# Two attention stages: the order of VectorE's work around the softmax maximum, and ScalarE for the last step of the layer norm

## The chip, the cores and the metric

The kernel runs on one core of a Trainium2 chip. It is one program with six stages. The metric is the device time of one execution in microseconds (us), the median of several runs. The engines of the core run side by side, each through its own instruction list in order, and wait for each other with semaphores: PE (TensorE, matmuls; PEld is its weight load), DVE (VectorE), ACT (ScalarE), POOL (GpSimd), and SP, which issues DMAs.

## The reference

32 batches of 128 rows of 128 values pass through six blocks; after each of them the block's output is added to its input and layer-normed without gain or bias. Two of the blocks are softmax attentions with 16 heads of 8 values, and the change is in these two:

```python
# stage 1: self-attention with rotary positions and a causal mask
scores = jnp.einsum('bhqd,bhkd->bhqk', Q, K) * scale
scores = jnp.where(causal_mask, -jnp.inf, scores)
attn = jax.nn.softmax(scores, axis=-1)
...
x = _layernorm(x + _L0_attn_ref(x, ...), axis=-1)
...
# stage 5: cross-attention, 77 keys from ctx_1024, a bias table and a padding mask
probs = jax.nn.softmax(scores, axis=-1)
out = jnp.einsum('bhts,bhsd->bhtd', probs, v)
...
x = _layernorm(x + _L1_xattn_ref(x, ctx_1024, ...), axis=-1)

def _layernorm(x, axis=-1, eps=1e-05):
    m = jnp.mean(x, axis=axis, keepdims=True)
    v = jnp.var(x, axis=axis, keepdims=True)
    return (x - m) / jnp.sqrt(v + eps)
```

## The kernel before

One function, `attention`, writes both stages; `cross` tells them apart (tile names begin with `a_` in the self-attention and `k_` in the cross-attention). The 32 batches are worked in 8 groups of 4, and the softmax of a group in 8 units: a unit is 8 heads of one batch, 128 query rows with 8 x 128 scores (self) or 8 x 77 scores (cross). I write "unit 0'" for a unit of the next group.

A unit passes through the engines like this. PE computes the scores into one of two pairs of PSUM banks (L660, in the self-attention with a mask added by L663). DVE takes the row maximum `mx` (L481) and subtracts it into `DD` (L483), so that the bank pair is free. ACT takes the exponential `E` (L370). PE transposes it (L670), ACT copies the transposed probabilities `PT` out of PSUM (L411), and PE multiplies them with the values for each batch (L680). DVE also sums each unit's exponentials into `sm` (L492); in the self-attention POOL first folds the two halves of `E` into `HS` (L280). The scores of unit u + 2 stand behind the transposes of unit u in PE's list, so each unit's chain feeds the next but one.

At the end of a group DVE takes the reciprocal `rr` of all 64 sums (L550), POOL spreads it to `rx` (L356), PE transposes that (L743), ACT copies it (L461), DVE multiplies it with the output into `oT` (L565), PE projects (L754), and DVE adds the residual into `Y` (L572), takes mean and variance (L72, L75), and, after POOL has computed the reciprocal deviation `rs` (L82, L84), writes the normed rows into `X` (L90, `ln_apply`: four instructions of 128 x 128).

No scheduler is involved. The order of each engine's list is the order in which `prelude` and `body` issue it; `schedule` (L223) runs the groups, the first two of the cross-attention written out, then pairs in a loop, then the last two. Beside the softmax, each group prepares the next one: transposed rows, projected keys, queries and values (in the self-attention with four rotary products `R` on DVE, L504; in the cross-attention with ACT writing the queries in four pieces `QM`, L400). In the cross-attention each group also computes the router logits of the group before: PE transposes its normed rows (L625), ACT copies them (L392), PE multiplies (L632), and DVE writes them to `LA` (L497).

Of the kernel before, what the change touches and what calls it, by code (L numbers as in the profile page):

```python
# [20 lines left out]
P = 128  # L21
# [80 lines left out]

LN_SEMS = "st mv lv rs"
# [62 lines left out]
def attention(c, tag, cross, W, wsem, wcount, xsem=None, first=None, gate=None):  # L166
# [11 lines left out]
    s = c.sems(tag, "xs xTp xT kp rot q k bd vp v z zv s_ready mx ma d e sm rr ex rTp ptp pt o_ready oT yp yr y2 xw cs cTp cT rc qf bf bl ql pf pw pd hs xTl xL lg la " + LN_SEMS)  # L178
# [44 lines left out]
    def schedule(eng, prelude, body):  # L223

        prelude()
        if cross and eng is nc.tensor:
            for g in range(NG):
                body(g, g % 2, min(2, NG - 1 - g))
            return
        if cross:  # L230
            body(0, 0, 2)
            body(1, 1, 2)
        with eng.Fori(1 if cross else 0, NG // 2 - 1) as i:
            body(i * 2, 0, 2)
            body(i * 2 + 1, 1, 2)
        body(NG - 2, 0, 1)
        body(NG - 1, 1, 0)
# [4 lines left out]
    with nc.Block() as block:  # L242
# [27 lines left out]
        def _(pool):  # L270
# [58 lines left out]
            def body(g, par, left):  # L329
# [31 lines left out]
                ln_rstd(pool, nc, ln, s, g + 1)  # L361
# [4 lines left out]
        def _(act):  # L366
# [53 lines left out]

            def prelude():
                if first is not None:
                    first["act"](act)
                nc.scalar.preload_act_table_set("exp_and_others")
                act.sem_inc(s["o_ready"], 1)
                if cross:
                    act.wait_ge(wsem, wcount)
                    nc.scalar.copy(QM[:, 0].rearrange("p g (b q) -> p g b q", b=GB), W["qc"][:, :, :].rearrange("p g (o q) -> p g o q", o=1).to_broadcast([D, 4, GB, P])).then_inc(s["qf"], 1)
                x_transposed(0)
                act.wait_ge(wsem, wcount)  # L430
                if cross:
# [12 lines left out]

            def body(g, par, left):
                for u in range(1, UN):
                    slot(g, u, left)
                    if left:
# [7 lines left out]
                        elif u == 6:  # L456
                            values(g + 1, 1 - par)
                    if cross and u == 5 and earlier(g):
# [11 lines left out]
        def _(dve):  # L470

            def less_max(g, par, u):
                hf, b = u % 2, u // 2
                at = g * UN + u + 1
                d = DD[:, u % 2].rearrange("p (i j) k -> p i j k", i=2)
                m = mx[:, u % 2, :].rearrange("p (i j) -> p i j", i=2)
                mb = mx[:, u % 2, :].rearrange("p (i j o) -> p i j o", i=2, o=1).to_broadcast([P, 2, HG, KL])
                dve.wait_ge(s["s_ready"], at)
                if not (isinstance(g, int) and g == 0 and u < 2):
                    dve.wait_ge(s["e"], at - 2)  # L480
                nc.vector.tensor_reduce(m, units(hf), AX_X, ALU.max).then_inc(s["mx"], 1)  # L481
                dve.wait_ge(s["mx"], at)
                nc.vector.tensor_tensor(d, units(hf), mb, ALU.subtract).then_inc(s["d"], 1)  # L483
# [30 lines left out]
            def prelude():  # L514
# [19 lines left out]
                less_max(0, 0, 0)  # L534
                less_max(0, 0, 1)
                sums(0, 0)
                less_max(0, 0, 2)
                sums(0, 1)
                if not cross:
                    rotate(1, 0)  # L540
# [848 lines left out]
def state_space(c, W, wsem, wcount, Wr, rsem, rcount):  # L1389
# [40 lines left out]
    ln, iln = c.ln, {k: (c.sb("m_i" + k, v.shape, F32, ctx) if k not in ("half", "eps") else v) for k, v in c.ln.items()}  # L1430
# [856 lines left out]
def program(nc, dram, out):  # L2287
    ctx = ExitStack()
    with ctx:
# [6 lines left out]
                "rs": c.sb("ln_rs", [P, GB]), "half": c.sb("ln_half", [P, GB]), "eps": c.sb("ln_eps", [P, GB])}  # L2296
# [39 lines left out]
        def first_dve(dve):  # L2336
            nc.vector.memset(c.warm[:, :], 1.0).then_inc(s_warm, 1)
            nc.vector.memset(c.ln["eps"][:, :], EPS)
            nc.vector.memset(c.ln["half"][:, :], -0.5)

# [123 lines left out]
```

## Time and profile before

| what | value |
|---|---|
| median of 3 runs | 1926.71 us (1925.93 to 1927.08) |
| span of the profiled execution | 1948.6 us; its own time is given only as this span, 21.9 us (1.1%) above the median of the runs |
| PE busy | 1562.9 us (80%) |
| DVE busy | 1491.3 us (77%) |
| ACT busy | 953.5 us (49%) |
| POOL busy | 920.7 us (47%) |
| self-attention, one group in the middle | 34.9 to 35.0 us (eight groups, from 0 to 308 us) |
| cross-attention, one group in the middle | 29.2 to 29.3 us (eight groups, from 1298 to 1556 us) |

The profile is one execution of the program taken by the hardware profiler. Busy shares over the whole span say little, since the six stages have different limits. The two stages of the change together take about 570 us of the span. A group is measured here from the start of one addition of the residual (`Y`, L572) to the next.

### The profile page before, as it was taken

Reading aid. Unit: us, or ns where it says so; the run is one execution under the profiler, and the core shown is the slowest. Engines: PE = TensorE matmul, PEld = TensorE weight load, DVE = VectorE, ACT = ScalarE, POOL = GpSimd, SP = SyncE. Lnnn points to the kernel's source line nnn. Section 1 sums busy time; section 2 is a strip of 40 time slices with the busy share of each in tenths; the row PEclk is TensorE's granted clock in tenths of the full one; section 3 lists DMA queues with packets and bytes.
Section 4 is the critical chain, followed back from the end, with each engine's and each line's share of the span. In section 5 each row is a group of like instructions: output and inputs, shape, how many; then the busy total and the mean of one; then the engine's idle time right before and its main releaser. Section 6 shows DMA issues by size and latency. Waiting matters only on the chain. (4 is left out here: it accounts for less than half of the span.)

```text
span 1948.6 us, 31799 instructions
## 1 busy us (share of the span) xinstructions
PE 1562.9 (80%) x10219; PEld 1017.4 (52%) x10219; DVE 1491.3 (77%) x2947; ACT 953.5 (49%) x1491; POOL 920.7 (47%) x938
## 2 busy tenths in 40 slices
PE   8889888989699978977878878769998811699991
PEld 4545547988476632322333333236776611588891
DVE  6899986887488779999989999967777678533335
ACT  3545543575544567657656666436566410011114
POOL 4455442444200147677676677654344100366653
PEclk8999998999899989999988999979999855799996
DMA  4000000000000000000000000020000040466654
GB/s 144 2 0 0 0 1 27 2 2 1 12 1 0 1 1 1 1 1 0 0 1 0 0 0 1 1 78 11 5 9 5 3 145 0 159 209 206 212 171 135
DMA packets 49075, 75.34 MB, mean 39 GB/s; under 512 B 8861, under 2 KB 34821, under 8 KB 48437
## 3 DMA queue, kind: packets, MB, share of 16 engines
q1 hardware_dynamic: 43541, 64.12, 10.5%
q0 software_dynamic: 4544, 9.32, 1.6%
q8 instruction: 67, 1.10, 0.2%
q14 instruction: 59, 0.48, 0.1%
q10 hardware_dynamic: 864, 0.33, 0.1%
HBM read 62.26 MB, written 11.48 MB: 38 GB/s over the span
## 5 line engine op out<-in xcount | busy, mean ns | idle before, releaser
L1506 POOL TENSOR_TENSOR m_hC<-m_h,m_Cs 128x512 f32<-128x512 f32 x256 | 328.2, 1287 | 169.2 <-DVE m_h L1680 122.6
L1788 PE MATMUL PS<-m_hC,identf 128*128 128x512 f32 x512 | 296.5, 662 | 100.9 <-POOL m_hC L1506 99.9
L1680 DVE TENSOR_TENSOR_SCAN m_h<-m_dA,PS 128x512 f32<-128x512 f32 x256 | 312.4, 1220 | 11.2
L1788 PEld LDWEIGHTS PS<-m_hC,identf 128*128 128x128 f32 x512 | 93.0, 203 | 236.4 <-POOL m_hC L1506 208.9
L1675 DVE TENSOR_TENSOR PS<-PS,m_DU 128x512 f32<-128x512 f32 x256 | 178.4, 697 | 19.9 <-issue 3.8
L1616 ACT ACTIVATE m_dA<-m_DT,m_A 128x508 f32<-128x508 f32 x256 | 174.3, 714 | 31.3 <-DVE m_DT L1664 31.1
L1996 ACT ACTIVATE e_Sg<-PS 128x512 f32<-128x512 f32 x71 | 42.4, 597 | 223.0 <-PE PS L2238 178.8
L2238 PE MATMUL PS<-e_xT,e_WT 128*128 128x128 f32 x1136 | 143.8, 281 | 4.9 <-DVE e_xT L2146 3.4
L1608 ACT COPY m_Cs<-PS 128x512 f32<-128x512 f32 x128 | 73.7, 576 | 143.7 <-PE PS L1766 143.5
L2238 PEld LDWEIGHTS PS<-e_xT,e_WT 128*128 128x128 f32 x1136 | 135.4, 195 | 9.3 <-DVE e_xT L2146 7.1
L1935 POOL DMA_INDIRECT e_XG<-token_rows,e_ids x71 | 68.8, 969 | 138.9 <-DVE e_ids L2140 117.6
L2153 DVE TENSOR_TENSOR e_HT<-PS,e_Sg 128x512 f32<-128x512 f32 x71 | 49.0, 691 | 81.6 <-PE PS L2238 73.5
L82 POOL TENSOR_TENSOR ln_lv<-ln_mv,ln_eps 128x4 f32<-128x4 f32 x24 | 4.8, 200 | 223.9 <-DVE ln_mv L75 223.9
L280 POOL TENSOR_TENSOR a_HS<-a_E 128x512 f32<-128x512 f32 x56 | 71.2, 1271 | 74.7 <-ACT a_E L370 74.7
L1940 POOL DMA_INDIRECT expert_rows<-e_Yo,e_ids x71 | 70.0, 985 | 72.2 <-DVE e_Yo L2159 60.6
L411 ACT COPY a_PT<-PS 128x1024 f32<-128x1024 f32 x63 | 63.8, 1012 | 73.8 <-PE PS L670 73.8
L411 ACT COPY k_PT<-PS 77x1024 f32<-77x1024 f32 x63 | 63.5, 1008 | 67.7 <-PE PS L670 67.5
L370 ACT ACTIVATE a_E<-a_DD 128x1024 f32<-128x1024 f32 x64 | 67.7, 1058 | 54.1 <-DVE a_DD L483 53.6
L670 PE MATMUL PS<-identf,a_E 128*128 128x128 f32 x512 | 71.6, 285 | 22.6 <-ACT a_E L370 22.3
L303 POOL TENSOR_TENSOR k_BD<-k_kT,w_hmask 32x1232 f32<-32x1232 f32 x32 | 71.5, 2233 | 36.3 <-ACT k_kT L387 30.4
L481 DVE TENSOR_REDUCE a_mx<-PS 128x8 f32<-128x1024 f32 x64 | 77.4, 1210 | 11.8 <-PE PS L663 11.6
L660 PE MATMUL PS<-k_BD,k_QM 128*128 128x308 f32 x256 | 80.8, 439 | 4.1 <-POOL k_BD L303 2.2
(411 smaller groups left out, 3801.6 us busy)
## 6 DMA issues: line engine op xcount, KB each, us to landing
e_WT<-in_w_wgu SPq DMA_DIRECT2D x71, 512.0 KB
token_rows<-X SPq DMA_DIRECT2D x2, 2048.0 KB
e_Y<-expert_rows SPq DMA_DIRECT2D x16, 256.0 KB, 4.0
k_BD<-in_w_bcr SPq DMA_DIRECT2D x1, 2464.0 KB, 9.5
e_w_wd<-in_w_wd SPq DMA_DIRECT2D x1, 2048.0 KB, 7.9
out_dram<-X SPq DMA_DIRECT2D x8, 256.0 KB, 2.4
X<-in_x SPq DMA_DIRECT2D x1, 1792.0 KB, 8.7
x_Cs<-in_ctx SPq DMA_DIRECT2D x8, 154.0 KB
```

The costliest lines, as they stand in the source:

```text
L303: nc.gpsimd.tensor_tensor(BD[r, par, gp].rearrange("p j b k -> p j (b k)"), flat(kT[r, :, :]).rearrange("p (o n) -> p o n", o=1).to_broadc ...
L411: nc.scalar.copy(PT[:, u % NP], PS[0:KL, 4:6, :].rearrange("p i (h q) -> p (i h) q", q=P)).then_inc(s["pt"], 1)
L481: nc.vector.tensor_reduce(m, units(hf), AX_X, ALU.max).then_inc(s["mx"], 1)
L660: ins = nc.tensor.matmul(scores(gp), q, BD[r, par, gp, :, b, :] if cross else BD[r, par, :, b, :], start=True, stop=cross)
L670: ins = nc.tensor.transpose(PS[0:KL, 4 + h // 4, (h % 4) * P:(h % 4 + 1) * P], E[:, u % NE, h, :], c.identf[:, :])
L1506: nc.gpsimd.tensor_tensor(hC[:, i % ND, :], hst[:, i % ND, :], Cs[:, n % ND, :], ALU.mult).then_inc(s["hC"], 1)
L1608: nc.scalar.copy(Cs[:, n % ND, :], bank(3)).then_inc(s["Cs"], 1)
L1616: nc.scalar.activation(dA[:, i % NA, :, 1:P], bl(DT[:, par, ch, :])[:, :, 1:P], ACT.Exp, scale=A[:, ch, n:n + 1]).then_inc(s["dA"], 1)
L1675: nc.vector.tensor_tensor(bank(4), bank(1 + n % 2), DU[:, par, ch, :], ALU.mult).then_inc(s["dBu"], 1)
L1680: nc.vector.tensor_tensor_scan(hst[:, i % ND, :], dA[:, i % NA].rearrange("p b l -> p (b l)"), bank(4), 0.0, ALU.mult, ALU.add).then_inc(s ...
L1788: nc.tensor.matmul(bank(5 + ch), c.identf[:, :], hC[:, i % ND, :], start=False, stop=(n == NS - 1)).then_inc(s["yacc"], 1)
L2238: ins = nc.tensor.matmul(PS[:, banks[i % 2], f * P:(f + 1) * P], WT[:, i % RW, w, f * P:(f + 1) * P], xT[:, i % 2, :], start=True, stop=True)
```

## The change

`less_max` is split. A new `maximum` takes the row maximum, and `less_max` is left with the subtraction, which now also carries the wait for the exponential of two units earlier. Between the two, VectorE's list now holds other work: in the self-attention a rotary product and the sums of an earlier unit, in the cross-attention the sums. The sums of unit u - 1 move from behind the subtraction of unit u to ahead of that of unit u + 1. At the end of a group the maximum of unit 0' is taken ahead of the last two sums.

The last step of the layer norm, `ln_apply` on VectorE, becomes `norm` on ScalarE (scale by `rs`, bias by `nb`) for all groups but the last. It is issued in the group after, behind the exponential of unit 4. GpSimd's `ln_scale` computes the additional `nb` = -mean x `rs` with two more operations on 128 x 4 values. VectorE waits for ScalarE (`xw`) before it writes `Y` again. The self-attention's first two groups are now also written out ahead of the loop.

```diff
+def ln_scale(pool, nc, ln, s, n):
+    pool.wait_ge(s["mv"], n)
+    nc.gpsimd.tensor_tensor(ln["lv"][:, :], ln["mv"][:, :, 1], ln["eps"][:, :], ALU.add).then_inc(s["lv"], 1)
+    nc.gpsimd.tensor_tensor(ln["ng"][:, :], ln["mv"][:, :, 0], ln["minus"][:, :], ALU.mult).then_inc(s["ng"], 1)
+    pool.wait_ge(s["lv"], n)
+    nc.gpsimd.tensor_tensor(ln["rs"][:, :], ln["lv"][:, :], ln["half"][:, :], ALU.pow).then_inc(s["rs"], 1)
+    pool.wait_ge(s["rs"], n)
+    pool.wait_ge(s["ng"], n)
+    nc.gpsimd.tensor_tensor(ln["nb"][:, :], ln["ng"][:, :], ln["rs"][:, :], ALU.mult).then_inc(s["nb"], 1)
...
-        if cross:
-            body(0, 0, 2)
-            body(1, 1, 2)
-        with eng.Fori(1 if cross else 0, NG // 2 - 1) as i:
+        body(0, 0, 2)
+        body(1, 1, 2)
+        with eng.Fori(1, NG // 2 - 1) as i:
...
-                ln_rstd(pool, nc, ln, s, g + 1)
+                if left:
+                    ln_scale(pool, nc, ln, s, g + 1)
+                else:
+                    ln_rstd(pool, nc, ln, s, g + 1)
...
+            def norm(g):
+                act.wait_ge(s["nb"], g + 1)
+                for b in range(GB):
+                    ins = nc.scalar.activation(X[:, bass.ds(g * GB + b, 1), :].rearrange("p o d -> p (o d)"), Y[:, b, :], ACT.Identity, scale=ln["rs"][:, b:b + 1], bias=ln["nb"][:, b:b + 1])
+                ins.then_inc(s["xw"], 1)
...
+                    if u == 3 and earlier(g):
+                        norm(g - 1)
...
-            def less_max(g, par, u):
+            def maximum(g, u):
+                dve.wait_ge(s["s_ready"], g * UN + u + 1)
+                nc.vector.tensor_reduce(mx[:, u % 2, :].rearrange("p (i j) -> p i j", i=2), units(u % 2), AX_X, ALU.max).then_inc(s["mx"], 1)
+            def less_max(g, u):
...
             def body(g, par, left):
-                for u in range(2, UN):
-                    if u + 1 < UN:
-                        less_max(g, par, u + 1)
-                        sums(g, u)
-                    else:
-                        sums(g, u)
-                        dve.wait_ge(s["sm"], g * UN + UN)
-                        nc.vector.reciprocal(rr[:, :], sm[:, :]).then_inc(s["rr"], 1)
-                        if left:
-                            less_max(g + 1, 1 - par, 0)
-                            less_max(g + 1, 1 - par, 1)
-                    if left:
-                        if cross:
-                            if u == 5:
-                                values(g + 1, 1 - par)
-                        elif u <= 4:
-                            rotate(g + 1, u - 1)
+                for u in range(2, UN - 1):
+                    maximum(g, u + 1)
+                    if left and not cross and u <= 5:
+                        rotate(g + 1, u - 2)
+                    if u >= 3:
+                        sums(g, u - 1)
+                    less_max(g, u + 1)
+                    if left and cross and u == 5:
+                        values(g + 1, 1 - par)
                     if cross and u == 6 and earlier(g):
                         logits(g - 1)
+                if left:
+                    maximum(g + 1, 0)
+                sums(g, UN - 2)
+                sums(g, UN - 1)
+                dve.wait_ge(s["sm"], g * UN + UN)
+                nc.vector.reciprocal(rr[:, :], sm[:, :]).then_inc(s["rr"], 1)
+                if left:
+                    less_max(g + 1, 0)
+                    maximum(g + 1, 1)
+                    less_max(g + 1, 1)
...
+                if earlier(g):
+                    dve.wait_ge(s["xw"], g)
                 nc.vector.tensor_tensor(flat(Y[:, :, :]), bank(AUX), flat(XB[:, :, :] if cross else group(c, g)), ALU.add).then_inc(s["yr"], 1)
                 dve.wait_ge(s["yr"], g + 1)
                 ln_stats(dve, nc, Y, ln, s, g + 1)
                 if left:
-                    less_max(g + 1, 1 - par, 2)
+                    maximum(g + 1, 2)
                     sums(g + 1, 1)
-                    if left == 2 and not cross:
-                        rotate(g + 2, 0)
-                ln_apply(dve, nc, group(c, g), Y, ln, s, g + 1, s["xw"])
+                    less_max(g + 1, 2)
+                else:
+                    ln_apply(dve, nc, group(c, g), Y, ln, s, g + 1, s["xw"])
```

Three places of the instruction lists are shown, all in the second group of the cross-attention, which is written out in both kernels.

The first is on VectorE at the end of a group, from the subtraction of unit 7 on. `LA` is the logits of the group before, the `k_sm` rows are the sums, the `k_rr` row is the reciprocal, and the `k_mx` and `k_DD` rows behind it belong to units 0' and 1'. Before:

```order
L483 TENSOR_TENSOR k_DD<-PS,k_mx 128x616
L492 TENSOR_REDUCE k_sm<-k_E 128x8
L497 TENSOR_SCALAR LA<-PS 128x32
L492 TENSOR_REDUCE k_sm<-k_E 128x8
L550 RECIPROCAL k_rr<-k_sm 128x64
L481 TENSOR_REDUCE k_mx<-PS 128x8
L483 TENSOR_TENSOR k_DD<-PS,k_mx 128x616
L481 TENSOR_REDUCE k_mx<-PS 128x8
L483 TENSOR_TENSOR k_DD<-PS,k_mx 128x616
```

The same place on VectorE after the change:

```order
L505 TENSOR_TENSOR k_DD<-PS,k_mx 128x616
L519 TENSOR_SCALAR LA<-PS 128x32
L497 TENSOR_REDUCE k_mx<-PS 128x8
L514 TENSOR_REDUCE k_sm<-k_E 128x8 x2
L582 RECIPROCAL k_rr<-k_sm 128x64
L505 TENSOR_TENSOR k_DD<-PS,k_mx 128x616
L497 TENSOR_REDUCE k_mx<-PS 128x8
L505 TENSOR_TENSOR k_DD<-PS,k_mx 128x616
```

Between the logits and the reciprocal there was one sum; now there are the maximum of unit 0' and two sums.

The second place is on VectorE behind the statistics of the layer norm, with the maximum and the subtraction of unit 2' and the sums of unit 1'. Before:

```order
L72 BN_STATS ln_st<-k_Y 128x6 x4
L75 BN_AGGR ln_mv<-ln_st 128x2 x4
L481 TENSOR_REDUCE k_mx<-PS 128x8
L483 TENSOR_TENSOR k_DD<-PS,k_mx 128x616
L492 TENSOR_REDUCE k_sm<-k_E 128x8
L90 TENSOR_SCALAR X<-k_Y,ln_mv,ln_rs 128x128 x4
```

The same place on VectorE after the change:

```order
L72 BN_STATS ln_st<-k_Y 128x6 x4
L75 BN_AGGR ln_mv<-ln_st 128x2 x4
L497 TENSOR_REDUCE k_mx<-PS 128x8
L514 TENSOR_REDUCE k_sm<-k_E 128x8
L505 TENSOR_TENSOR k_DD<-PS,k_mx 128x616
```

The sums of unit 1' moved ahead of the subtraction of unit 2', and the four instructions that write `X` are gone.

The third place is on ScalarE, behind the copy `k_PT` of unit 3 and the exponential `k_E` of unit 4. Before:

```order
L411 COPY k_PT<-PS 77x1024
L370 ACTIVATE k_E<-k_DD 128x616
L400 ACTIVATE k_QM<-PS,w_bq 32x512 x4
L411 COPY k_PT<-PS 77x1024
L370 ACTIVATE k_E<-k_DD 128x616
```

The same place on ScalarE after the change:

```order
L425 COPY k_PT<-PS 77x1024
L384 ACTIVATE k_E<-k_DD 128x616
L414 ACTIVATE k_QM<-PS,w_bq 32x512 x4
L439 ACTIVATE X<-k_Y,ln_nb,ln_rs 128x128 x4
L425 COPY k_PT<-PS 77x1024
L384 ACTIVATE k_E<-k_DD 128x616
```

The four new instructions stand between the four query pieces and the copy of unit 4, with the exponential of unit 5 behind that.

## Rows read from the trace of the kernel before

**Rows 1.** The head of the page: the span of the profiled execution.

```profile
span 1948.6 us, 31799 instructions
```

**Rows 2.** Stretches, a group each: length, busy PE PEld DVE ACT POOL, granted clock, DMA.

```profile
165.10:200.08 34.98, 31.53 (x272) 17.83 (x272) 32.04 (x44) 17.89 (x19) 18.11 (x18) 1.00 0.00 0
1348.10:1377.40 29.30, 26.41 (x268) 20.86 (x268) 23.14 (x44) 18.35 (x25) 13.04 (x9) 1.00 0.03 8
1406.66:1435.89 29.23, 26.42 (x268) 20.84 (x268) 23.14 (x44) 18.34 (x25) 13.03 (x9) 1.00 0.03 7
```

**Rows 3.** Waits over five cross-attention groups: total us, times, longest.

```profile
DVE LA L497 <- PE PS L632: 7.2, 5, 1.5
```

**Rows 4.** Timeline of VectorE in a cross-attention group: start, duration, instruction, idle before.

```profile
1408.63 0.77 DVE L481 TENSOR_REDUCE k_mx<-PS 128x8 f32<-128x616 f32 x1
1409.43 0.80 DVE L483 TENSOR_TENSOR k_DD<-PS,k_mx 128x616 f32<-128x616 f32 x1
1410.14 0.78 DVE L492 TENSOR_REDUCE k_sm<-k_E 128x8 f32<-128x616 f32 x1
1410.85 1.11 DVE L90 TENSOR_SCALAR X<-k_Y,ln_mv,ln_rs 128x128 f32 x4
...
1428.52 0.19 DVE L497 TENSOR_SCALAR LA<-PS 128x32 f32 x1 [1.44 <-PE PS L632]
1428.63 0.79 DVE L492 TENSOR_REDUCE k_sm<-k_E 128x8 f32<-128x616 f32 x1
1429.44 0.55 DVE L550 RECIPROCAL k_rr<-k_sm 128x64 f32<-128x64 f32 x1
```

**Rows 5.** Timeline of TensorE in the same group: transposes of units 2 and 5, of `rx`.

```profile
1411.12 1.07 PE L670 MATMUL PS<-identf,k_E 128*77 128x128 f32 x8 [0.88 <-ACT k_E L370]
...
1422.57 1.10 PE L670 MATMUL PS<-identf,k_E 128*77 128x128 f32 x8
...
1431.29 0.60 PE L743 MATMUL PS<-identf,k_rx 128*128 128x128 f32 x4
```

**Rows 6.** Timeline of ScalarE in the same group: queries, copy of unit 4, exponential of unit 5.

```profile
1417.72 2.75 ACT L400 ACTIVATE k_QM<-PS,w_bq 32x512 f32<-32x512 f32 x4 [0.27 <-PE PS L609]
1420.50 1.01 ACT L411 COPY k_PT<-PS 77x1024 f32<-77x1024 f32 x1
1421.53 0.72 ACT L370 ACTIVATE k_E<-k_DD 128x616 f32<-128x616 f32 x1
```

**Rows 7.** Timeline of ScalarE in stage 4, where it norms rows.

```profile
796.54 1.50 ACT L1630 ACTIVATE X<-PS,m_no,ln_rs 128x128 f32 x4 [1.87 <-POOL m_no L1516]
797.92 1.33 ACT L1616 ACTIVATE m_dA<-m_DT,m_A 128x508 f32<-128x508 f32 x2
```

**Rows 8.** Timeline of GpSimd in the same cross-attention group.

```profile
1430.08 1.04 POOL L356 TENSOR_TENSOR k_rx<-k_rr,k_one 128x512 f32<-128x512 f32 x1 [4.73 <-DVE k_rr L550]
```

**Rows 9.** Timeline of VectorE in a self-attention group.

```profile
135.73 2.19 DVE L90 TENSOR_SCALAR X<-a_Y,ln_mv,ln_rs 128x128 f32 x4
...
154.65 0.68 DVE L492 TENSOR_REDUCE a_sm<-a_HS 128x8 f32<-128x512 f32 x1
156.08 1.22 DVE L492 TENSOR_REDUCE a_sm<-a_E 128x8 f32<-128x1024 f32 x1 [0.76 <-ACT a_E L370]
157.34 0.55 DVE L550 RECIPROCAL a_rr<-a_sm 128x64 f32<-128x64 f32 x1
157.81 1.16 DVE L481 TENSOR_REDUCE a_mx<-PS 128x8 f32<-128x1024 f32 x1
```

**Rows 10.** Timeline of TensorE in the same self-attention group.

```profile
141.45 1.09 PE L670 MATMUL PS<-identf,a_E 128*128 128x128 f32 x8 [1.13 <-ACT a_E L370]
...
154.96 0.60 PE L663 MATMUL PS<-w_cmask,identb 128*128 128x512 bf16 x2
...
161.37 1.09 PE L670 MATMUL PS<-identf,a_E 128*128 128x128 f32 x8 [0.64 <-ACT a_E L370]
```

**Rows 11.** Timeline of TensorE in the last cross-attention group.

```profile
1528.18 1.92 PE L670 MATMUL PS<-identf,k_E 128*77 128x128 f32 x8 [2.58 <-ACT k_E L370]
```

More of the change, by code:

```diff
@@ L177, in attention @@
     EXPERTS, SK_EPS = 8, 0.05
-    s = c.sems(tag, "xs xTp xT kp rot q k bd vp v z zv s_ready mx ma d e sm rr ex rTp ptp pt o_ready oT yp yr y2 xw cs cTp cT rc qf bf bl ql pf pw pd hs xTl xL lg la " + LN_SEMS)
+    s = c.sems(tag, "xs xTp xT kp rot q k bd vp v z zv s_ready mx ma d e sm rr ex rTp ptp pt o_ready oT yp yr y2 xw cs cTp cT rc qf bf bl ql pf pw pd hs xTl xL lg la ng nb " + LN_SEMS)
     ctx = ExitStack()
@@ L470, in _ @@
         def _(dve):
-            def less_max(g, par, u):
-                hf, b = u % 2, u // 2
+            def maximum(g, u):
+                dve.wait_ge(s["s_ready"], g * UN + u + 1)
+                nc.vector.tensor_reduce(mx[:, u % 2, :].rearrange("p (i j) -> p i j", i=2), units(u % 2), AX_X, ALU.max).then_inc(s["mx"], 1)
+            def less_max(g, u):
                 at = g * UN + u + 1
-                d = DD[:, u % 2].rearrange("p (i j) k -> p i j k", i=2)
-                m = mx[:, u % 2, :].rearrange("p (i j) -> p i j", i=2)
                 mb = mx[:, u % 2, :].rearrange("p (i j o) -> p i j o", i=2, o=1).to_broadcast([P, 2, HG, KL])
-                dve.wait_ge(s["s_ready"], at)
                 if not (isinstance(g, int) and g == 0 and u < 2):
                     dve.wait_ge(s["e"], at - 2)
-                nc.vector.tensor_reduce(m, units(hf), AX_X, ALU.max).then_inc(s["mx"], 1)
                 dve.wait_ge(s["mx"], at)
-                nc.vector.tensor_tensor(d, units(hf), mb, ALU.subtract).then_inc(s["d"], 1)
+                nc.vector.tensor_tensor(DD[:, u % 2].rearrange("p (i j) k -> p i j k", i=2), units(u % 2), mb, ALU.subtract).then_inc(s["d"], 1)
             def sums(g, u):
@@ L533, in prelude @@
                     dve.wait_ge(xsem[1], 16)
-                less_max(0, 0, 0)
-                less_max(0, 0, 1)
+                maximum(0, 0)
+                less_max(0, 0)
+                maximum(0, 1)
+                less_max(0, 1)
+                maximum(0, 2)
                 sums(0, 0)
-                less_max(0, 0, 2)
+                less_max(0, 2)
                 sums(0, 1)
-                if not cross:
-                    rotate(1, 0)
             def body(g, par, left):
-                for u in range(2, UN):
-                    if u + 1 < UN:
-                        less_max(g, par, u + 1)
-                        sums(g, u)
-                    else:
-                        sums(g, u)
-                        dve.wait_ge(s["sm"], g * UN + UN)
-                        nc.vector.reciprocal(rr[:, :], sm[:, :]).then_inc(s["rr"], 1)
-                        if left:
-                            less_max(g + 1, 1 - par, 0)
-                            less_max(g + 1, 1 - par, 1)
-                    if left:
-                        if cross:
-                            if u == 5:
-                                values(g + 1, 1 - par)
-                        elif u <= 4:
-                            rotate(g + 1, u - 1)
+                for u in range(2, UN - 1):
[7 more added lines that the diff above has]
+                        values(g + 1, 1 - par)
                     if cross and u == 6 and earlier(g):
                         logits(g - 1)
+                if left:
[8 more added lines that the diff above has]
+                    less_max(g + 1, 1)
                 dve.wait_ge(s["rc"], g + 1)
@@ L1429, in state_space @@
     hC = sb("hC", [P, ND, T])
-    ln, iln = c.ln, {k: (c.sb("m_i" + k, v.shape, F32, ctx) if k not in ("half", "eps") else v) for k, v in c.ln.items()}
+    ln, iln = c.ln, {k: (c.sb("m_i" + k, v.shape, F32, ctx) if k not in ("half", "eps") else v) for k, v in c.ln.items() if k not in ("ng", "nb", "minus")}
     bank = lambda i, r=P: PS[0:r, i, :]
@@ L2295, in program @@
         c.ln = {"st": c.sb("ln_st", [P, GB, 6]), "mv": c.sb("ln_mv", [P, GB, 2]), "lv": c.sb("ln_lv", [P, GB]),
-                "rs": c.sb("ln_rs", [P, GB]), "half": c.sb("ln_half", [P, GB]), "eps": c.sb("ln_eps", [P, GB])}
+                "rs": c.sb("ln_rs", [P, GB]), "ng": c.sb("ln_ng", [P, GB]), "nb": c.sb("ln_nb", [P, GB]), "minus": c.sb("ln_minus", [P, GB]), "half": c.sb("ln_half", [P, GB]), "eps": c.sb("ln_eps", [P, GB])}
         c.PS = ctx.enter_context(nc.psum_tensor("PS", [P, 8, 512], F32))
@@ L2339, in first_dve @@
             nc.vector.memset(c.ln["half"][:, :], -0.5)
+            nc.vector.memset(c.ln["minus"][:, :], -1.0)
         def first_pe(pe):
```

## The prediction, made before the changed kernel ran

> **What bounds the kernel now.** I read the head of the page first [rows 1]: the profiled execution spans 1948.6 us, 21.9 us more than the median of the runs. The sum below is made of differences between stretches of this execution, and I set it against the median one to one, since the two stages' groups repeat to a tenth of a us. A measurement of this kernel can tell some 0.2% (3.9 us) from no change.
>
> Next the busy time by stretch [rows 2]. The reader should see how different the two stages are. A self-attention group takes 34.98 us, of which VectorE works 32.04 and TensorE 31.53: both are close to full. A cross-attention group takes 29.23 us; there TensorE works 26.42 and VectorE only 23.14. VectorE has 6 us of idle time in it, TensorE 2.8. The granted clock is 1.00 (2.4 GHz) in all three, and the second stretch, written out in straight lines, is no slower than the third, a pass of the loop, by more than 0.07 us; so I cost the two self-attention groups that are now written out at nothing.
>
> Then the list of waits in the cross-attention: VectorE waits 1.4 to 1.5 us in each group for the router logits before it may write `LA` [rows 3]. Last the timelines of one group, engine by engine, to see which wait ends last. TensorE's row of the `rx` transposes shows no wait in it [rows 5]: TensorE runs without a pause from the transposes of unit 6 to the end of the group, so what makes TensorE late in this stage makes the group late. That is the test for each edit.
>
> **The change in the cross-attention.** Three moved pieces can reach TensorE.
>
> First, the sums of unit 1' now stand ahead of the subtraction of unit 2'. Before, the maximum began at 1408.63 and the subtraction at 1409.43 [rows 4]. The subtraction (0.80 long) is followed by independent work 0.71 after its start, while a maximum of about the same length holds its reader for 0.80: the separation is worth 0.09. The new order puts the maximum (0.77, so 0.69 until the next starts) and the sums (0.71) ahead: 1408.63 + 0.69 + 0.71 = 1410.03, so the subtraction comes 0.60 later. Its exponential, and the transposes of unit 2, are waited for by TensorE already (0.88 at 1411.12 [rows 5]), and everything behind them in TensorE's list moves too. **+0.6 per group.**
>
> The Trainium skill, in "VectorE: DVE Perf Modes", section "The DRAIN you can't avoid", says that VectorE flushes after every operation and that a semaphore between chained operations costs nothing extra; by this, standing other work between saves nothing, and the term would be 0.7. The trace's 0.09 disagrees with it here, by little.
>
> Second, ScalarE's new step. It is the same operation as stage 4's, scale and bias from a column each, on 128 x 128, four times: 1.50 us, and the next instruction starts 1.38 after its start [rows 7]. That one reads PSUM and this one SBUF, which the row does not show. From below I bound it by VectorE's four instructions for the same work, 1.11 [rows 4], from above by four without overlap: each overlaps the next by 1.50 - 1.38 = 0.12, so 1.38 + 4 x 0.12 = 1.86. I take 1.38, the nearest row. It stands behind the four query pieces, which end at 1420.47, and ahead of the copy of unit 4, which began at 1420.50 with no idle time before it [rows 6]: ScalarE is already late there. Behind the copy is the exponential of unit 5, which ended at 1421.53 + 0.72 = 1422.25, and TensorE took that unit's transposes at 1422.57 without a wait [rows 5]. The slack is 0.27 after the 0.05 of a hand-over. 1.38 - 0.27: **+1.1 per group.**
>
> Third, the reciprocal. VectorE wrote `LA` at 1428.52, then one sum, and took the reciprocal at 1429.44 [rows 4]. Now the maximum of unit 0' (0.71) and a further sum (0.71) stand between, because they follow the logits, whose wait does not get shorter: TensorE issues them late. The reciprocal comes 1.42 later. GpSimd's `rx` follows it, 1430.08 to 1431.12 [rows 8], and TensorE transposed that at 1431.29 [rows 5]: slack 0.12 after the hand-over. **+1.3 per group.** What is late next hangs on TensorE: the transposed reciprocals, the product `oT`, the projection, `Y`. The subtraction of unit 0' comes only 0.65 later than before and hides behind that.
>
> These three add, since each delays TensorE from a point at which it then runs on or waits in order: 3.0 us in each of the six intervals in which a group's logits, queries and successor all exist, 18.0 us. The first and the last group have neither the second nor the third (no logits or no queries), but the first: 0.3 to 0.6 each, 0.9 together. VectorE's 1.02 of `ln_apply` (1410.85, 1.11 long [rows 4]) comes off an engine that then waits for TensorE: nothing. The new wait of VectorE for ScalarE ahead of `Y` is over more than 10 us earlier; behind it stands the whole layer norm, so it would cost its full length if the cover went. GpSimd's two more small operations delay only its copy of rows, and it waited 4.73 us in front of `rx` [rows 8].
>
> **The change in the self-attention.** VectorE gives up 2.19 per group [rows 9] and some 0.09 in each of seven separated pairs. TensorE is the one to ask again. It waited 1.13 for the exponential of unit 3 [rows 10], behind `ln_apply`: that wait goes. The subtraction of unit 2' comes 0.5 later, as above (sums of 0.68, less the overlap and the 0.09). TensorE is 0.6 ahead from there and runs on without a wait until the scores of unit 0', which ended at 154.96 + 0.60 = 155.56 and now end at 154.9. VectorE now takes the maximum of unit 0' there (1.1 until the next starts), then the sums of unit 6 (0.6) and those of unit 7 (1.26 until the reciprocal may start, 156.08 to 157.34 [rows 9]): the reciprocal is at 157.9, 0.5 later than before. So the lead is lost at `rx`. Afterwards TensorE no longer waits its 0.64 for the exponential of unit 0' [rows 10], whose subtraction now follows the reciprocal at once instead of after the maximum (157.81). 0.64 - 0.5 leaves 0.1 to 0.3; I take 0.2, seven times: **-1.4.** The bounds: both waits recovered, 1.77 per group; or nothing. ScalarE's new step lies in a stage where ScalarE is busy 17.89 of 34.98 [rows 2], and I put it at nothing; if it were uncovered it would cost 1.38 per group.
>
> **Sum.** 18.0 + 0.9 - 1.4 = +17.5 us: 1926.7 + 17.5 = 1944.2 us, 0.9% slower.
>
> **The rivals.**
>
> VectorE is the bound in both stages (faster). Then what is taken off it comes off the time: 2.1 and 0.6 in seven self-attention groups, 1.0 and 0.6 in seven cross-attention groups, 30 us, 1896 us. For it speaks VectorE's 32.04 of 34.98; against it the 23.14 of 29.23 [rows 2]. It decides at TensorE's idle time: if that does not grow beyond 2.8 us in a cross-attention group, this one is right. Chance 0.07. The Trainium skill, in "Perfetto Trace Analysis", section "Optimizing Scalar/DVE Operations", says that where VectorE is saturated, giving work to ScalarE may make sense; by that rule's condition the trace agrees in the self-attention only.
>
> The cross-attention's delays fall into the 2.8 us in which TensorE waits anyway (no change): 1926.7 - 1.4 = 1925.3 us. Against it: at the transposes of unit 5 and of `rx` there is no wait to fall into [rows 5]. Chance 0.07.
>
> The self-attention recovers both of TensorE's waits: 1.77 instead of 0.2, seven times, 11 us better, 1933.2 us. For it: VectorE has nearly 3 us less to do. Against it: the reciprocal stands behind a maximum that waits for scores. Chance 0.12.
>
> The clock falls. After a wait of 2.58 us TensorE's transposes took 1.92 instead of 1.1 in the last group [rows 11], that is 1.2 GHz; the scores behind them double too, some 1.7 us for one such dip. The longer waits of TensorE could bring one in each of six groups: +10, 1954.4 us. Against it: each single wait stays below 1.6 us, and the waits of 0.88 and 1.13 left the clock at 1.00 [rows 2]. Chance 0.10.
>
> **How the numbers follow.** My forecast has 0.64, with a range of its own of 1938 to 1949: ScalarE's step at 1.11 or 1.86 gives -1.6 or +2.9 in six groups, the self-attention's ends +1.4 or -3 within this case. The predicted time is 1944.2. The range, to take in the recovery in the self-attention and nearly all of the clock's case, is 1933 to 1954. Slower by over 0.2%: 0.64 + 0.12 + 0.10 = 0.86; within 0.2%: 0.07; faster: 0.07.
>
> **What the profile after would show.** Middle groups of the cross-attention of about 32.2 us instead of 29.2, of the self-attention of about 34.8. TensorE waiting about 1.5 us for the exponential of unit 2 and about 1 us each for that of unit 5 and for `rx`, where there was 0.88, nothing and nothing. ScalarE's four instructions at about 1.5 us, right between the queries and a copy that does not wait. VectorE idle for 8 us or more in a cross-attention group. The prediction is wrong if ScalarE's step turns out far shorter than 1.1, if the logits come early enough for the reciprocal, or if self-attention groups fall to 33 us.

## The result, and the profile after

The changed kernel takes **1945.93 us** (median of 4, 1944.83 to 1950.64) against 1926.89 us (median of 4, 1925.93 to 1929.99) for the kernel before on the same chip: ratio 1.0104, 95% interval 1.0093 to 1.0116, 1.0% slower. The forecast was 1944.2 us, 1933 to 1954.

The two profiled spans can't be compared: the first execution of the kernel before [rows 1] spent 396.9 us behind its last `Y`, where every other profile here has 369 to 373. So I compare the stretches between additions of the residual (`Y`), in two profiles of each kernel:

| stretch, us | before | after |
|---|---|---|
| a middle self-attention interval | 34.9 to 35.0 | 34.45 to 34.73 |
| last self-attention interval | 33.90, 35.50 | 35.47, 35.46 |
| a middle cross-attention interval | 29.23 to 29.31 | 32.45 to 32.58 |
| last cross-attention interval | 28.08, 28.10 | 31.11, 31.12 |
| all seven of the self-attention | 243.5, 245.0 | 242.5, 242.5 |
| all seven of the cross-attention | 203.62, 203.66 | 226.25, 226.25 |

The seven intervals of the cross-attention lose 22.6 us, those of the self-attention give back 0.9 to 2.5. The first cross-attention group, which no interval holds, loses 0.8: from its first transposes of `E` to its `Y` it took 30.93 and 30.99 us before, and 31.78 twice after. That makes 20.9 to 22.5 us, more than the 19.0 between the medians. Where the other 2 to 3.5 us came back is not shown: the stretch from the self-attention's last `Y` to the cross-attention's first, nearly all of it stages that the change doesn't touch, took 1040 to 1050 us in the profiles of this study.

The windows of the profile after, with the columns of [rows 2], are a stretch as long as a self-attention group, a cross-attention group and the last cross-attention interval:

```profile
165.59:200.05 34.46, 31.33 (x273) 17.91 (x272) 29.25 (x39) 19.12 (x23) 18.44 (x20) 1.00 0.00 0
1414.95:1447.48 32.53, 26.68 (x268) 20.78 (x268) 21.58 (x40) 19.97 (x29) 13.36 (x11) 1.00 0.02 7
1545.05:1576.16 31.11, 24.94 (x229) 19.28 (x229) 17.30 (x31) 13.44 (x19) 3.77 (x6) 0.79 0.00 1
```

In the cross-attention group VectorE works 1.6 us less and idles 11 us; TensorE does the same work in 3.3 us more, and its idle time grows from 2.8 to 5.9 us. Its timeline in that group has the three waits (the last bracket) where [rows 5] had 0.88, none and none:

```profile
1419.99 1.07 PE L697 MATMUL PS<-identf,k_E 128*77 128x128 f32 x8 [1.45 <-ACT k_E L384]
...
1432.81 1.07 PE L697 MATMUL PS<-identf,k_E 128*77 128x128 f32 x8 [1.30 <-ACT k_E L384]
...
1442.82 0.66 PE L770 MATMUL PS<-identf,k_rx 128*128 128x128 f32 x4 [1.16 <-POOL k_rx L367]
```

VectorE's timeline shows the cause of the first and the third, to be read against [rows 4]: the sums between maximum and subtraction, and the maximum and two sums between `LA` and the reciprocal.

```profile
1416.92 0.77 DVE L497 TENSOR_REDUCE k_mx<-PS 128x8 f32<-128x616 f32 x1
1417.60 0.78 DVE L514 TENSOR_REDUCE k_sm<-k_E 128x8 f32<-128x616 f32 x1
1418.30 0.79 DVE L505 TENSOR_TENSOR k_DD<-PS,k_mx 128x616 f32<-128x616 f32 x1
...
1438.73 0.19 DVE L519 TENSOR_SCALAR LA<-PS 128x32 f32 x1 [1.57 <-PE PS L659]
1438.86 0.80 DVE L497 TENSOR_REDUCE k_mx<-PS 128x8 f32<-128x616 f32 x1
1439.58 1.49 DVE L514 TENSOR_REDUCE k_sm<-k_E 128x8 f32<-128x616 f32 x2
1441.10 0.55 DVE L582 RECIPROCAL k_rr<-k_sm 128x64 f32<-128x64 f32 x1
```

ScalarE's timeline shows the cause of the second, to be read against [rows 6]: the norm holds the copy of unit 4 and the exponential of unit 5 back by 1431.04 - 1429.37 = 1.67 us.

```profile
1426.59 2.75 ACT L414 ACTIVATE k_QM<-PS,w_bq 32x512 f32<-32x512 f32 x4 [0.27 <-PE PS L636]
1429.37 1.65 ACT L439 ACTIVATE X<-k_Y,ln_nb,ln_rs 128x128 f32 x4
1431.04 1.01 ACT L425 COPY k_PT<-PS 77x1024 f32<-77x1024 f32 x1
1431.95 0.72 ACT L384 ACTIVATE k_E<-k_DD 128x616 f32<-128x616 f32 x1
```

### The profile page after: what moved, and what is told of

Read it like the earlier page. It is cut to its first block and busy times, and to the rows that moved or that the text cites. A ratio compares the mean times of both kernels' runs of the same rounds, so it can differ in the third digit from the quotient of the medians.

```text
span 1947.8 us, 31764 instructions
## 1 busy us (share of the span) xinstructions
PE 1555.3 (80%) x10219; PEld 1016.8 (52%) x10219; DVE 1462.8 (75%) x2892; ACT 973.9 (50%) x1547; POOL 925.3 (48%) x966
## 3 DMA queue, kind: packets, MB, share of 16 engines
q8 instruction: 71, 1.16, 0.2%
## 5 line engine op out<-in xcount | busy, mean ns | idle before, releaser
L1643 ACT ACTIVATE m_dA<-m_DT,m_A 128x508 f32<-128x508 f32 x256 | 174.3, 714 | 34.3 <-DVE m_DT L1691 31.1
L497 DVE TENSOR_REDUCE k_mx<-PS 128x8 f32<-128x616 f32 x64 | 50.8, 793 | 62.7 <-PE PS L687 62.6
L697 PE MATMUL PS<-identf,k_E 128*77 128x128 f32 x512 | 71.6, 285 | 23.9 <-ACT k_E L384 23.9
```

The source lines that it names most:

```text
L497: nc.vector.tensor_reduce(mx[:, u % 2, :].rearrange("p (i j) -> p i j", i=2), units(u % 2), AX_X, ALU.max).then_inc(s["mx"], 1)
L697: ins = nc.tensor.transpose(PS[0:KL, 4 + h // 4, (h % 4) * P:(h % 4 + 1) * P], E[:, u % NE, h, :], c.identf[:, :])
L1643: nc.scalar.activation(dA[:, i % NA, :, 1:P], bl(DT[:, par, ch, :])[:, :, 1:P], ACT.Exp, scale=A[:, ch, n:n + 1]).then_inc(s["dA"], 1)
```

## The experiments

The theory: three separate delays of TensorE (late subtraction, norm on ScalarE, late reciprocal) make the cross-attention slow, and they add. Against it: one of them alone, ScalarE's added work as such, or VectorE as the bound. Group times are those of middle groups. A ratio is to the kernel before, with its 95% interval.

**Each part alone.** `order_only` has the new order with the norm back on VectorE (and GpSimd's `ln_rstd` in every group); against the changed kernel:

```diff
...
-                    if u == 3 and earlier(g):
-                        norm(g - 1)
...
-                if earlier(g):
-                    dve.wait_ge(s["xw"], g)
...
-                else:
-                    ln_apply(dve, nc, group(c, g), Y, ln, s, g + 1, s["xw"])
+                ln_apply(dve, nc, group(c, g), Y, ln, s, g + 1, s["xw"])
```

`norm_only` has the old order with the norm on ScalarE (with GpSimd's `ln_scale`, and the first two self-attention groups written out as in the change); against the kernel before:

```diff
...
+                    if u == 3 and earlier(g):
+                        norm(g - 1)
...
+                if earlier(g):
+                    dve.wait_ge(s["xw"], g)
...
-                ln_apply(dve, nc, group(c, g), Y, ln, s, g + 1, s["xw"])
+                else:
+                    ln_apply(dve, nc, group(c, g), Y, ln, s, g + 1, s["xw"])
```

> VectorE's new order alone; the last step of the layer norm is back on VectorE in every group, ScalarE has none of it. My theory (TensorE is made late at three separate places of a middle cross-attention group: 0.57 us at the transposes of unit 2, 1.37 at those of unit 5, 1.28 at those of the reciprocals): the first and the third remain, the second goes, so a cross-attention group takes about 31.1 us against 29.25 before and 32.5 after, and a self-attention group is not better than before (34.9 to 35.1), since there the reciprocal is later and the norm's 2.1 us are back on VectorE; time about 1941 to 1943 us. Rival S (all the loss comes from ScalarE's new step, the late reciprocal only follows from it): cross-attention groups of 29.3, time 1925 to 1928. Rival V (all the loss comes from VectorE's order): groups of 32.5, time 1946 or more.

> VectorE's order is that of before (maximum and subtraction side by side, sums behind), and ScalarE does the last step of the layer norm at the place of the change. My theory: in the cross-attention only the second delay remains, a middle group takes 30.3 to 30.6 us; in the self-attention VectorE gives up 2.2 us per group and its reciprocal is not later, so a group falls to about 33.6 us against 34.95 before and 34.5 after. Time 1922 to 1927 us. Rival S: cross-attention groups of 32.5, time 1940 or more. Rival V: cross-attention groups of 29.3.

Measured, `order_only`: 1933.21 us (ratio 1.0044, 1.0027 to 1.0062), cross group 31.1 to 31.2, self group 34.45. The cross-attention was as expected (29.25 + 1.9), the self-attention was not: the new order alone gives all of the 0.5 us. The time came 8 us below the expected 1941 to 1943. Part of that is the self-attention (about 0.5 us a group) and the last cross-attention interval, 27.64 us instead of the changed kernel's 31.11; the rest was not followed up. `norm_only`: 1924.16 us (0.9989, 0.9979 to 1.0000), cross 30.6 (29.25 + 1.35; one of 30.93), self 33.66 to 33.85, as expected. So in the self-attention the norm on ScalarE is worth 1.2 us in the old order and nothing in the new one (why: the last experiment).

**Each delay undone in the cross-attention alone**, against the changed kernel. `norm_early` issues the norm one unit earlier:

```diff
-                    if u == 3 and earlier(g):
+                    if u == (2 if cross else 3) and earlier(g):
```

`recip_back` puts the logits behind the sums of unit 6 and the maximum of unit 0' behind the reciprocal:

```diff
-                    if cross and u == 6 and earlier(g):
-                        logits(g - 1)
-                if left:
+                if left and not cross:
                     maximum(g + 1, 0)
                 sums(g, UN - 2)
+                if cross and earlier(g):
+                    logits(g - 1)
...
+                if left and cross:
+                    maximum(g + 1, 0)
```

`sum_behind` has the subtraction of unit 2' ahead of the sums of unit 1':

```diff
-                    sums(g + 1, 1)
-                    less_max(g + 1, 2)
+                    if cross:
+                        less_max(g + 1, 2)
+                        sums(g + 1, 1)
+                    else:
+                        sums(g + 1, 1)
+                        less_max(g + 1, 2)
```

`three_back` has all three edits.

> The change, but in the cross-attention ScalarE does the norm one unit earlier, behind the copy of the keys, where it waited 1.44 us for TensorE's transposes of unit 3; the self-attention is as in the change. My theory: the second delay goes (TensorE's transposes of unit 5 no longer wait), the two others remain: groups of 31.1 to 31.3 us, time about 1938 us. Rival S: groups of 29.3, time 1926. Rival V: groups of 32.5, time 1946.

> The change, but at the end of a cross-attention group VectorE's order is that of before: sums of unit 6, logits, sums of unit 7, reciprocal, and only then the maximum of unit 0 of the next group. My theory: the third delay goes (TensorE's transposes of the reciprocals no longer wait), groups of 31.2 us, time about 1938 us. Rival S: unchanged, groups of 32.5, time 1946. Rival V: groups of 30.0 or less, since only 0.6 of VectorE's new order is left.

> The changed kernel with the three subtractions and sums at the end of a cross group in the old order (subtraction of the next group's unit 2 ahead of the sums of its unit 1); nothing else differs. If the late subtraction is what makes TensorE wait for the transposes of unit 2, that wait falls from 1.45 to about 0.9 us, a middle cross group from 32.5 to 31.8 to 32.0 us, and the time from 1946 to 1941.5 to 1943 us. Rival, VectorE's own work sets the group: the order of two of its instructions changes nothing, the group stays at 32.5 us and the time at 1946 us.

> The changed kernel with all three suspected delays undone in the cross attention alone (subtraction before sums, reciprocal in its old place, ScalarE's norm one unit earlier); the norm stays on ScalarE and the self attention is as changed. If the three delays are the whole loss, a middle cross group is 29.2 to 29.5 us (before 29.25), a self group 34.45 to 34.7 us, and the time 1923 to 1928 us. Rival, the norm on ScalarE costs something by itself wherever it stands, since ScalarE has 1.65 us more to do in each group: the group stays at 30.5 us or more and the time at 1934 us or more.

| kernel | time, us | ratio to before | cross group, us | TensorE's three waits, us |
|---|---|---|---|---|
| after | 1945.93 | 1.0104 (1.0093 to 1.0116) | 32.5 | 1.45, 1.30, 1.16 |
| norm_early | 1938.73 | 1.0054 (1.0032 to 1.0075) | 31.2 | 1.45, none, 1.16 |
| recip_back | 1938.15 | 1.0055 (1.0038 to 1.0071) | 31.15 | 1.45, 1.31, none |
| sum_behind | 1942.14 | 1.0076 (1.0057 to 1.0094) | 32.0 | 0.95, 1.30, 1.15 |
| three_back | 1930.41 | 1.0004 (0.9990 to 1.0017) | 29.3 | 0.95, none, none |

Each edit takes away its own wait and leaves the others. They are worth 1.3, 1.4 and 0.5 us, and together 3.2: they add. A window of `three_back` has the group at 29.30 us, with ScalarE still doing the norm (19.75 us busy instead of 18.34):

```profile
1411.47:1440.77 29.30, 26.42 (x268) 20.84 (x268) 21.67 (x41) 19.75 (x29) 13.37 (x11) 1.00 0.03 7
```

So ScalarE's 1.4 us of added work cost nothing by themselves; their place did. `three_back`'s time missed the expected 1923 to 1928: its profiled execution (1933.49 us) took 1050.1 us between the two attentions' additions, where that of the changed kernel took 1045.2, and 30.59 in the last interval, below. Why the other runs are long too is not shown; the ten lie between 1923.1 and 1933.5.

**The last groups.** A piece is a row of TensorE's timeline, some matrix products of one kind. In the changed kernel's last cross-attention interval TensorE waits 3.37 us and then runs five pieces at 1.2 GHz. Before, the wait was 2.58 us [rows 11] and two pieces were slow:

```profile
1550.37 1.96 PE L697 MATMUL PS<-identf,k_E 128*77 128x128 f32 x8 [3.37 <-ACT k_E L384]
1552.12 2.26 PE L687 MATMUL PS<-k_BD,k_QM 128*128 128x308 f32 x4
1554.31 1.94 PE L707 MATMUL PS<-k_PT,k_V 77*32 77x128 f32 x32
1556.18 1.99 PE L697 MATMUL PS<-identf,k_E 128*77 128x128 f32 x8
1557.96 2.15 PE L687 MATMUL PS<-k_BD,k_QM 128*128 128x308 f32 x4
1559.97 1.07 PE L697 MATMUL PS<-identf,k_E 128*77 128x128 f32 x8
```

`warm_last` adds dummy products to that wait (and to the self-attention's) in TensorE's list of the changed kernel; two further runs repeat the kernels.

```diff
+                    if u == 2 and not left:
+                        pe.wait_ge(s["yr"], g)
+                        keep_warm(c, 14, AUX)
```

> The changed kernel, and in the last group of either attention TensorE does 14 dummy matrix products, into a bank that nobody reads, while it waits for the transposes of unit 2 (added work, the result is untouched). If the last intervals are long because TensorE's clock falls after the wait of 3.37 us, the granted clock of the last cross-attention interval rises from 0.79 to 0.95 or more, that interval falls from 31.1 to 26.5 to 27.5 us, the last self-attention interval from 35.5 to 31 to 33 us; the middle groups stay at 32.5 and 34.5 us; the time falls by 4 to 7 us to 1939 to 1942 us. Rival, the last groups are long by their order alone: the two intervals stay within 1 us and so does the time, or it grows by the products.

> The changed kernel once more, for one profile. If it is chance how many of TensorE's pieces run at 1.2 GHz after the wait in the last cross-attention group, that interval differs from the first profile's 31.1 us, anywhere from 26.3 to 31.5 us, while the middle groups repeat at 32.45 to 32.58 us. If the length of the wait alone sets it, the interval is 31.1 us again.

> The kernel before once more, for one profile. Middle groups 34.9 and 29.25 us again; the last cross-attention interval anywhere from 25.5 to 28.1 us if the slow pieces are chance, 28.1 us if they are set by the wait. The part behind the last Y of the cross-attention, 396.9 us in the first profile and 370 to 372 us in all the other kernels', should come to 370 us, and the span to about 1923 us.

`warm_last`: 1939.63 us (1.0062, 1.0046 to 1.0079). Its two last intervals:

```profile
270.18:301.71 31.53, 25.19 (x239) 14.95 (x240) 21.98 (x31) 15.33 (x18) 9.77 (x11) 0.94 0.00 1
1545.97:1573.17 27.20, 23.41 (x241) 17.50 (x243) 17.39 (x31) 13.34 (x19) 3.78 (x6) 0.96 0.01 2
```

That is 3.9 us less in each, at a clock of 0.94 and 0.96, with middle groups unchanged: the clock it is. How many pieces run slowly the length of the wait alone does not say. After 2.58 us `norm_only` had none slow, as its row shows; after 2.86 `three_back` had five, `sum_behind` two, the second of them in part:

```profile
1529.55 1.07 PE L696 MATMUL PS<-identf,k_E 128*77 128x128 f32 x8 [2.58 <-ACT k_E L384]
```

The repeated profiles gave 31.12 and 28.10 again in the cross-attention, but `before_again`'s last self-attention interval took 35.50 us where the first had 33.90: after the same wait of 3.29 us six pieces were slow instead of four. Its span was 1929.8 us, not the expected 1923 (the part behind the last `Y` was 372.8, near the expected 370). The Trainium skill, "TensorE: Matmul & The Clock Gate", section "Part 1: The HAM clock gate (the "warmup" mystery)", says of a kernel's start that the number of slow matmuls varies between runs of one kernel. The 33.90 and 35.50 are a like difference behind a wait, and the two equal pairs don't show one.

**A version that beats both.** `no_early` is the old order with the norm on ScalarE, in the cross-attention a unit earlier; `best2` adds the dummy products of `warm_last`. `no_early` against `norm_only`:

```diff
-                    if u == 3 and earlier(g):
+                    if u == (2 if cross else 3) and earlier(g):
```

> The kernel before, in its old order of VectorE's work, with the norm's last step on ScalarE, in the cross attention one unit earlier than the change has it. By the theory of three separate delays, the self group is that of the run with the norm alone (33.66 to 33.85 us), the cross group loses that run's delay of 1.3 us and comes to 29.0 to 29.4 us, and the time is about 1924.2 - 6 * 1.4 = 1915.8 us, 1914 to 1918. Rival, an earlier norm delays the exps of units 3 and 4 as much as the later one did exp 5: cross group 30.5 us or more, 1923 us or more.

> The same as the run before it, and in the last group of either attention TensorE does 14 dummy matrix products, into a bank that nobody reads, while it waits for the transposes of unit 2 (added work, the result is untouched). If TensorE's clock falls there after a long wait, the granted clock of the last group rises and the two last intervals together lose 1 to 3 us: 1913 to 1915 us. Rival, the clock is not lost in this order, since the wait is short: no difference from the run before it, or up to 1 us longer by the products themselves.

`no_early`: 1919.51 us (0.9951, 0.9937 to 0.9966), self 33.66 to 33.85, cross 29.23 to 29.34 and one of 29.59, a little above the expected 29.4; the time is 1.5 us above its range. `best2`: **1914.68 us (0.9927, 0.9911 to 0.9942)**. Its last self-attention interval fell from 34.00 to 30.35, the last of the cross-attention only from 26.95 to 26.67; together they lost 3.9 us, more than the expected 1 to 3. In the cross-attention two pieces had been slow (1.96 and 1.81 us, the second in part), and the products took that away. But behind the products the transposes of unit 2 began 0.29 us later (4.81 us after `Y` instead of 4.52), and the projection that closes the group now ran at 1.2 GHz. First `no_early`, then `best2`:

```profile
1545.65 1.16 PE L780 MATMUL PS<-w_wo,k_oT 128*128 128x128 f32 x8 [0.88 <-DVE k_oT L588]
```

```profile
1539.65 2.08 PE L783 MATMUL PS<-w_wo,k_oT 128*128 128x128 f32 x8 [0.88 <-DVE k_oT L588]
```

There the same projection took 2.07 to 2.08 us in the kernel before, the changed kernel and `warm_last` too, and 1.16 in `norm_only`, `order_only` and `sum_behind`.

**What the self-attention gained.** VectorE's `ln_apply` took 2.19 us there [rows 9] and 1.11 in the cross-attention [rows 4], for four equal instructions. The list of groups for line 90 in the kernel before, with min/median/max in ns of one:

```profile
L90 DVE TENSOR_SCALAR X<-a_Y,ln_mv,ln_rs x32: 333/338/1418, 65.9 to 308.0; 128x128 f32 x24, 128x128 f32<-128x128 f32 x8
```

GpSimd's timeline of the kernel before at that place:

```profile
135.79 1.27 POOL L280 TENSOR_TENSOR a_HS<-a_E 128x512 f32<-128x512 f32 x1 [1.59 <-ACT a_E L370]
```

GpSimd's fold begins 0.06 us behind the start of the four (135.73), and 2.19 us fits one of 1.42 beside three of the median, each overlapping the next by 0.08. So it is in each of the first seven groups: one of the four took 1.22 to 1.42 us and ended 0.08 to 0.09 us behind the fold beside it. In the eighth, with no fold beside them, the four took 343 to 348 ns. In `order_only` the norm stands clear of the fold, takes 1.11, and TensorE's two waits in the group (1.04, 1.11) are those of the changed kernel: there the norm on VectorE costs nothing. `norm_up` is the kernel before with `ln_apply` moved up in the self-attention, clear of the fold:

```diff
                     less_max(g + 1, 1 - par, 2)
+                    if not cross:
+                        ln_apply(dve, nc, group(c, g), Y, ln, s, g + 1, s["xw"])
                     sums(g + 1, 1)
...
-                ln_apply(dve, nc, group(c, g), Y, ln, s, g + 1, s["xw"])
+                if cross or not left:
+                    ln_apply(dve, nc, group(c, g), Y, ln, s, g + 1, s["xw"])
```

> The kernel before, with one step of VectorE moved in the self-attention alone: the last step of the layer norm comes right behind the subtraction of unit 2', ahead of the sums and the rotary product instead of behind them, so that it starts about 1.2 us earlier and is over before GpSimd folds unit 2'. VectorE has the same work. If that step took 2.19 us instead of 1.11 because GpSimd's fold ran beside it, it falls to 1.1 us, TensorE's wait of 1.13 us for the exponential of unit 3 falls to about 0.1, and a middle self group goes from 34.95 to 33.8 to 34.0 us, the time from 1926.7 to 1918 to 1920 us. Rival, the step is slow whatever runs beside it (one stage's data or order): it stays at 2.2 us and the group at 34.9 us.

1920.19 us (0.9973, 0.9964 to 0.9982): the time is just above its range, the middle self groups of 33.82 to 33.96 are in theirs, and TensorE's wait for the exponential of unit 3 is gone. VectorE's timeline has the norm, over before GpSimd's next fold (168.16 to 169.43):

```profile
166.82 1.11 DVE L90 TENSOR_SCALAR X<-a_Y,ln_mv,ln_rs 128x128 f32 x4
```

The window of that group:

```profile
162.48:196.30 33.82, 31.53 (x272) 17.83 (x272) 30.88 (x43) 17.90 (x19) 18.11 (x18) 1.00 0.00 0
```

With all of the norm on VectorE the group is within 0.2 us of `norm_only`'s, which has it on ScalarE. It was the overlap with the fold that cost, and hardly the 1.11 us of the norm itself.

## Why the prediction was right, point by point

**The mechanism** stood: TensorE had no slack at the three places in the cross-attention, and each of the three moved pieces delays it. The rival of VectorE as the bound fell by its own sign, TensorE's idle time, which grew from 2.8 to 5.9 us; that of hidden delays fell with the three waits.

**The sizes of the three terms.** Late subtraction: +0.6 forecast, 1.45 - 0.88 = 0.57 by the wait and 0.5 by the undoing. Late reciprocal: +1.3 forecast, 1.3 to 1.4 by undoing. The norm: +1.1 forecast, 1.3 measured, because the step is 1.67 and not 1.38; the row in stage 4 [rows 7], which reads PSUM, was too short a model for a step that reads SBUF, though inside the bounds (1.11 to 1.86). The six middle intervals together grew by 19.6 us (175.5 to 195.1) where the prediction had 18.0. The Trainium skill, "ScalarE: Activation LUTs", section "What ACT_TABLE_LOAD costs", would have been nearer: 186 ns + 0.833 per column, 93 more for each pointer operand, and 93 of overlap make an estimate of 4 x (479 - 93) + 93 = 1637 ns, beside the trace's 1.65 us.

**The ends** were mis-sized: "0.3 to 0.6 each" against +0.8 in the first cross-attention group and +3.0 in the last interval. There the wait in front of unit 2's transposes grew by 0.79 us, and most of the rest goes with five slow pieces instead of two. That the clock falls after a longer wait was on record as a rival for the middle groups, where it did not happen (granted clock 1.00); in the last group, which dips already before [rows 11], the prediction did not apply it.

**The self-attention** was forecast at -0.2 per group and came to -0.45; the last interval is 35.5 as in one of the two profiles of before. TensorE's waits in the group of the window above:

```profile
171.82 1.09 PE L697 MATMUL PS<-identf,a_E 128*128 128x128 f32 x8 [1.04 <-ACT a_E L384]
194.92 0.66 PE L770 MATMUL PS<-identf,a_rx 128*128 128x128 f32 x4 [1.12 <-POOL a_rx L367]
```

The two waits of [rows 10] that the forecast let go are gone, and the lead is lost at `rx`, as it said. The first of the rows above is no new wait; in the group of [rows 10] it was

```profile
135.77 1.09 PE L670 MATMUL PS<-identf,a_E 128*128 128x128 f32 x8 [0.77 <-ACT a_E L370]
```

and these transposes of unit 2 came 0.46 us later behind `Y` than before, where the prediction had 0.5. The forecast gain was too small because of the reciprocal: TensorE was through with the scores of unit 0' 0.98 us earlier behind `Y` (24.38 instead of 25.36) and not 0.66, so the reciprocal came 0.26 us later (27.40 instead of 27.14) and not 0.5. The step that failed is the reason for the first wait: the prediction took `ln_apply`'s 2.19 as VectorE's load. `norm_up` shows that half of it was the overlap with GpSimd. The full recovery (33.2 us a group) did not come; the old order with the norm on ScalarE comes nearest, at 33.7.

**The number.** By stretches the change costs 20.9 to 22.5 us; the forecast summed up 17.5, with the norm and the ends too small. That the measured time came within 1.7 us of 1944.2 is in part luck: the 2 to 3.5 us that came back elsewhere are in no term of the sum.

**The separation itself** is worth what was estimated, 0.09 per pair: the next instruction starts 0.68 to 0.71 after its predecessor where a reader of it starts after 0.80 [rows 4]. The 0.7 us of work put between costs more wherever TensorE waits for the subtraction.

## What to carry to other kernels

Before filling a short stall on an engine that is not the bound, ask who waits for the instruction behind the stall: in the cross-attention 0.09 us a pair was saved, and 0.5 and 1.4 us a group were paid at the two places where TensorE stood behind the moved work. Work handed to an engine with idle time can be free or not by its place in that engine's list: in the cross-attention the same norm, one unit earlier, cost nothing instead of 1.3 us. And an instruction that takes twice as long in one stage as in another is to be looked at beside the other engines' timelines before its work is given away.

## What the runs showed of the hardware

A VectorE instruction of 128 x 128 (f32, scale and offset from columns, SBUF to SBUF) took 338 ns in the median and up to 1418 ns where GpSimd's 1.27 us addition began beside it; moved clear of it, 336 to 346 ns in all 32 of the self-attention. GpSimd's additions took 1.26 to 1.34 us either way. The Trainium skill, "Perfetto Trace Analysis", section "Optimizing Scalar/DVE Operations", says that the two engines share an SBUF read port, which an instruction of VectorE on two ports locks; the runs agree that the two hinder each other, and here it is VectorE's instruction that lasts longer; that a port is the reason no run here shows.

After waits of 2.58 to 3.75 us TensorE ran none to six pieces at 1.2 GHz, and equal waits gave different counts, in two executions of one kernel too (3.29 us, four and six). 14 dummy products (2.97 us for the 13 in the records) in the wait kept the pieces right behind it at 2.4 GHz, though not the projection at the end of the group, which in the cross-attention came behind two more waits (1.37 and 0.88 us). What decides the count was not settled.
